# Value tiles and three query groups as three products of rounded parts; the held chunk's work ahead of the last batch's cross units

## What is computed

```python
x = x + _L0_attn_ref(_layernorm(x, axis=-1), L0_attn_wq, L0_attn_wk, L0_attn_wv, L0_attn_wo)
x = x + _L0_xattn_ref(_layernorm(x, axis=-1), ctx_512, L0_xattn_Wq, L0_xattn_Wkv_expand, L0_xattn_Wout)
x = x + _L0_ffn_ref(_layernorm(x, axis=-1), L0_ffn_w_gate, L0_ffn_w_up, L0_ffn_w_down)
```

```python
h = jax.nn.silu(jnp.einsum('bsh,hi->bsi', x, w_gate)) * jnp.einsum('bsh,hi->bsi', x, w_up)
h_sparse = _sparsify_2to4(h)
return jnp.einsum('bsi,ih->bsh', h_sparse, w_down)
```

## Time and profile before

| | us |
|---|---|
| median of 3 executions | 415.29 (414.1 to 415.61) |
| the profiled execution, whole | 414.97 |
| its span, first to last instruction | 413.2 |
| PE busy | 392.2 (95% of the span) |
| DVE busy | 286.0 (69%) |
| ACT busy | 211.2 (51%) |
| POOL busy | 161.2 (39%) |

### The profile page before, as it was taken

How to read it: one execution, slowest core, us unless ns; L and a number is a source line. 1 busy time by engine, 2 the same in 40 slices (tenths; PEclk the granted TensorE clock), 3 DMA queues, 4 the chain that set the end, 5 groups by cost and what they waited for, 6 DMA issues and landing times.

```text
span 413.2 us, 7990 instructions
## 1 busy us (share of the span) xinstructions
PE 392.2 (95%) x2959; PEld 317.1 (77%) x2960; DVE 286.0 (69%) x607; ACT 211.2 (51%) x537; POOL 161.2 (39%) x160
## 2 busy tenths in 40 slices
PE   8997999899999999999999999999998999889996
PEld 7776778667699777777789877877786879757895
DVE  5977931788769972688859974688959961585373
ACT  1574731587334841486443752287544741777230
POOL 5562790378411420277611430167632500255000
PEclk9999999999999999999999999999999999988999
DMA  7985430303001300242000400342001300300000
GB/s 214 367 309 149 121 103 33 118 24 78 3 6 52 103 0 27 79 121 78 0 8 2 153 2 2 102 110 64 2 2 66 87 2 27 110 19 2 27 0 27
DMA packets 33446, 28.90 MB, mean 70 GB/s; under 512 B 18688, under 2 KB 28032, under 8 KB 33152
## 3 DMA queue, kind: packets, MB, share of 16 engines
q1 hardware_dynamic: 33408, 28.40, 22.2%
HBM read 19.21 MB, written 5.24 MB: 59 GB/s over the span
## 4 chain that ended last, share of the span: by engine, by line
PE 65%; DVE 16%; issue 6%; ACT 5%; POOL 4%; DMA 2%; SPq 1%; POOLq 0%; DVEq 0%; ACTq 0%
PE ps L593 13%; PE ps L462 13%; PE ps L658 9%; PE ps L534 8%; PE ps L674 3%; DVE mx L909 3%; PE ps L555 3%; PE ps L579 3%; PE ps L471 3%; ACT prob L1264 3%; POOL prob L1158 3%; DVE total L923 2%; PE ps L514 2%; PE ps L632 2%; DMA wqk_sb<-in_wqk 2%
## 5 line engine op out<-in xcount | busy, mean ns | idle before, releaser
L1158 POOL TENSOR_TENSOR prob<-prob,inv 128x512 f32<-128x512 f32 x80 | 84.4, 1060 | 84.6 <-DVE inv L929 84.5
L462 PE MATMUL ps<-xnT,wqk_sb 128*128 128x256 f32 x320 | 77.4, 384 | 1.1 <-DMA wqk_sb<-in_wqk 0.8
L462 PEld LDWEIGHTS ps<-xnT,wqk_sb 128*128 128x128 f32 x320 | 57.8, 190 | 11.6 <-issue 3.8
L1264 ACT ACTIVATE prob<-ps,mx 128x128 f32<-128x128 f32 (+1 forms) x128 | 52.5, 426 | 15.8 <-DVE mx L907 14.7
L1151 POOL TENSOR_TENSOR qs<-rope 128x512 f32<-128x512 f32 x32 | 40.7, 1271 | 43.1 <-DVE rope L879 39.1
L534 PE MATMUL ps<-ident_sb,prob 128*128 128x128 f32 x320 | 50.3, 282 | 5.2 <-POOL prob L1158 5.0
L1274 ACT ACTIVATE pT<-ps 128x512 f32<-128x512 f32 x80 | 47.6, 599 | 13.7 <-PE ps L534 13.2
L879 DVE TENSOR_TENSOR rope<-ps,trig_sb 64x512 f32<-64x512 f32 x70 | 48.2, 688 | 0.9
L534 PEld LDWEIGHTS ps<-ident_sb,prob 128*128 128x128 f32 x320 | 37.9, 143 | 13.2 <-POOL prob L1158 8.4
L1134 POOL TENSOR_TENSOR rstd<-vareps,power 128x1 f32<-128x1 f32 x24 | 13.2, 553 | 76.7 <-DVE vareps L858 76.5
L907 DVE TENSOR_REDUCE mx<-ps 128x2 f32<-128x512 f32 (+1 forms) x48 | 32.7, 689 | 10.0 <-PE ps L514 9.4
(11 more groups left out here) (145 smaller groups left out, 693.9 us busy)
## 6 DMA issues: line engine op xcount, KB each, us to landing
k<-kx SPq DMA_DIRECT2D x32, 128.0 KB, 2.9
q<-qx SPq DMA_DIRECT2D x32, 128.0 KB, 2.6
vb<-v_sb SPq DMA_DIRECT2D x42, 64.0 KB, 2.1
wqk_sb<-in_wqk SPq DMA_DIRECT2D x4, 512.0 KB, 8.2
work<-in_wgu SPq DMA_DIRECT2D x4, 512.0 KB, 9.6
wo_sb<-in_wo SPq DMA_DIRECT2D x1, 2048.0 KB, 15.7
vb<-v_sb SPq DMA_DIRECT2D x36, 32.0 KB, 2.4
wd_sb<-in_wd SPq DMA_DIRECT2D x1, 1024.0 KB, 6.1
```

The source lines that it names most:

```text
L462: mm = pe.matmul(o[:, half, :], wqk_sb[:, k, g, half, :], xnT[:, 0, k, :], start=(k == 0), stop=(k == KT - 1))
L1158: pool.tensor_tensor(p, p, inv[:, i % ND, 0:g].unsqueeze(2).broadcast_to([P, g, 512 // g]), ALU.mult).then_inc(s_norm, 1)
L1264: ins = act.activation(prob[:, i % ND, h * k:(h + 1) * k], ps[:, BANK_S + i % 2, h * k:(h + 1) * k], ACT.Exp, bias=mx[:, i % ND, h:h + 1], ...
```

## The change

**Three products.** From the second batch on, that is wherever b is not `None`, `v_tile` and the query groups 5, 6 and 7 (`SPLIT`) are computed in three products of float32r parts. The parts of the rows, `xs_hi` and `xs_lo`, lie in the buffers of the latent keys. ACT writes `xs_hi` and then `xnT` (`rows_parts`, in the place of `copy_norm`); DVE subtracts (`rows_rest`, behind `rank_sums` and ahead of `keep`, in batch 0 behind `normalise`). The parts of the weights are made in batch 0: five rounding copies on ACT (`half_weights`, one after each of the exponentials 3 to 7) and five subtractions on POOL (`rest_of_weights`), two ahead of the last four `split_weights` and three behind them.

**Held chunk.** In the last batch "up10" is multiplied between the scores of units 1 and 2 of the window (code of the batch before), gate and up of "11" ahead of `cross_norm(b, 0)`; DVE's comparisons and `keep` stand ahead of the cross units; `down(HELD, 0)` is done ahead of them and half of `down(HELD, 1)` after the second. Two and two `idle` products take places between the units. DVE copies the transposed probabilities of the first four cross units. A one-column exponential moves ACT's table load ahead.

**Space.** The context is loaded into both halves of the partitions, the two latent weights share a tile, and both window outputs lie in `qs`; the comparisons of the held chunk lie in `pT`.

```diff
+SPLIT = (5, 6, 7)
-IDLE = {"values": 1, "transposes": 1, "gates": 1, "ranks": 3, "last": 1}
-HELD_FIRST = {2: (1, 2), 4: (3,)}
-HELD_SECOND = {13: (0,), 14: (1,)}
+IDLE_UNITS = {13: 1, 14: 1}
+IDLE = {"scores": 2, "values": 1, "transposes": 1, "gates": 1, "ranks": 3, "last": 1}
+HELD_AT = 2
...
                 for half in halves:
+                    if b is not None and g in SPLIT:
...
+                        for k in range(KT):
+                            pe.matmul(o[:, half, :], wq_hi[:, k, j, half, :], xs_hi[:, k, :], start=(k == 0), stop=False)
+                            pe.matmul(o[:, half, :], wq_lo[:, k, j, half, :], xs_hi[:, k, :],
+                                      start=False, stop=False)
+                        for k in range(KT):
+                            mm = pe.matmul(o[:, half, :], wq_hi[:, k, j, half, :], xs_lo[:, k, :],
+                                           start=False, stop=(k == KT - 1))
...
                 if more:
-                    wait_drained(pe, "ln1", b)
                     v_tile("v0", b, 0)
                     window_out(b, 1, pair=0)
                 else:
-                    for j in range(2):
-                        gate_up(HELD, 1, j, ("gate",))
+                    gate_up(HELD, 1, 0, ("gate",))
+                    gate_up(HELD, 1, 1)
                 cross_norm(b, 0, n)
...
                 if not more:
-                    for j in range(2):
-                        gate_up(HELD, 1, j, ("up",))
+                    down(HELD, 0, (0, 1, 2))
                 cross_norm(b, 1, n)
...
                     if not more:
-                        if i in HELD_FIRST:
-                            down(HELD, 0, HELD_FIRST[i])
+                        if i == HELD_AT:
+                            down(HELD, 1, (0, 1))
+                        if i == HELD_AT + 1:
+                            wait_drained(pe, "up11", HELD)
+                            idle(IDLE["scores"], BANK_O)
...
                 if b == HELD:
-                    for i in range(HEAD):
-                        unit_scores(b + 1, i)
+                    unit_scores(b + 1, 0)
+                    unit_scores(b + 1, 1)
+                    gate_up(HELD, 1, 0, ("up",))
+                    unit_scores(b + 1, 2)
...
+                if c and b < HELD:
+                    rows_rest(b + 1)
                 dve.wait_ge(s_wins, FC * b + c + 1)
...
+            def unit_pT(b, i):
+                u = UNITS * b + i
+                dve.wait_ge(s_tr, u + 1)
+                dve.wait_ge(s_av, u - NPT + 1)
+                dve.tensor_copy(pT[:, i % NPT, :], ps[:, BANK_PT + i % 2, :]).then_inc(s_pTv, 1)
...
                 if b == 0:
+                    for k in range(KT):
+                        rest_of_weights(k)
                     for c in range(NQB - LATE, WCHUNKS):
                         split_weights(c)
+                    for k in range(len(SPLIT)):
+                        rest_of_weights(KT + k)
                 n = 3 * b + (3 if more else 2)
                 inverse_root(1, n, (0,))
...
+            def rows_parts(b):
+
+                wait_filled(act, "ln1", b)
+                act.wait_ge(s_kx, 32 * (b + 1))
+                act.activation(xs_hi[:], half_banks("ln1", b), ACT.Copy)
+                act.activation(xnT[:, 0], half_banks("ln1", b), ACT.Copy).then_inc(s_xhi, 1)
```

212 lines of the change are left out of this document (139 added, 73 removed).

## The result

The changed kernel took **421.12 us** (417.42 to 422.71, four executions) beside 415.21 of the kernel before: a ratio of 1.0138, with a 95% interval of 1.0103 to 1.0173. That is slower by 1.4%, and outside the predicted range, 412.8 to 419.2. The same kernel, measured three more times beside the kernel before, gave 1.0046 (1.0014 to 1.0077), 1.0082 (1.0064 to 1.0100) and 1.0077 (1.0047 to 1.0106), with medians of 417.49, 417.76 and 417.75. So two things have to be explained: the 3 us or so by which it is slower in most executions, and the 3.6 us more of the first measurement.

A forecast was written before the change was run, and what follows sets the result against it. PE was taken to bound the middle batches, while in the last batch's cross units it waits for ACT's exponentials. Sum: 414.97 − 2.2 + 3.8 + 1.3 − 1.15 = 416.7 us; range 412.8 to 419.2.

The forecast's parts named there:

- The products: Value tiles and query groups in batches 0 to 2 as three products of parts: −2.2 us, bounds 0 and −4.5.
- the groups: Query groups 5, 6 and 7 as products of parts: 0.55 us gained in each of three batches, −1.65.
- the value tiles: Value tiles as products of parts in batches 0 to 2: −0.75 us from v1, +0.2 cost at v0.
- v0: First value tile, before the first cross norm: gain nil, rows late, cost +0.1 us in batches 1 and 2.
- q7's second half: Second half of the last query group: only covers DVE's last normalisation, lands nothing; the first half lands 0.15 us.
- q5: Query group ahead of the transposes of units 9 and 10: gives 0.1 of its 0.30 us.
- q6: Query group covering ACT copies that move with PE: its 0.30 us lands in full.
- POOL's queue: Batch 0: nine subtractions delay the second norm's inverse root, so PE waits at `cross_norm(0, 0)`: +3.8 us, bounds 0 and 5.4.
- if PE finds rows ready there: Sign of being wrong: PE not waiting for DVE's rows at `cross_norm(0, 0)` in batch 0, where some 4 us idle was forecast.
- The clock behind the stall: Batch 0, after PE's wait: a stretch at 1.2 GHz costs +1.3 us, bounds 0 and 3.4.
- The last batch: Held chunk reordered, ACT paces the cross units: −1.95 us plus 0.8 for the clock, −1.15; bounds +0.8 and −3.5.
- slower by the second query tile: Rival: before the fifth cross unit, DMAs a microsecond later keep PE at 1.2 GHz; 419.1 us, chance 0.25.

The follow-up runs named there:

- seven_guarded: The guarded kernel: changed kernel, seven of POOL's nine subtractions moved behind the second norm's inverse root, POOL waiting for DVE before each piece; 410.12 us, 0.9887.
- groups_alone: seven_guarded with the value tiles back in float32, so only q5, q6 and q7 are products of parts; 412.01 us, 0.9919.
- root_first: Changed kernel, POOL's nine subtractions in batch 0 start only when DVE has normalised the next batch's rows; 418.39 us, 1.0092.
- before_seven: Kernel before, three more subtractions into unread tiles behind POOL's four in batch 0; 416.30 us, 1.0024.
- seven_behind_root: Changed kernel, seven of POOL's nine subtractions in batch 0 moved behind the second norm's inverse root, no waits added; 410.69 us, 0.9922.
- four_first: Changed kernel, POOL's nine reordered: the four of the gate weights first, then the two value parts and three of the query groups; 415.52 us, 1.0024.
- eight_lookups: Changed kernel, eight more SBUF to SBUF normalisations on DVE in batch 0 against POOL's nine subtractions, into unfilled tiles; 421.02 us, 1.0133.
- other_form: Changed kernel, DVE's normalisation of the second row tile of the next rows in batch 0 also writes its row sum to a spare tile; 417.97 us, 1.0094.
- after_third: Changed kernel without edit, measured a third time; 417.76 us, 1.0082.
- after_fourth: Changed kernel without edit, measured a fourth time; 417.75 us, 1.0077.
- guarded_again: seven_guarded without edit, measured again for its spread; 410.52 us, 0.9908.
- before_guarded: Kernel before, POOL's four subtractions of batch 0 held until DVE has normalised the next rows; 414.49 us, 0.9995.

## Why the prediction was wrong, and where it was right

*The products, −2.2.* Measured −2.0. The parts lay otherwise: the groups gave 1.05 where I had 1.65, and the value tiles 0.95 where I had 0.75 − 0.2 = 0.55. Of the value tiles, v0 gave nothing, as predicted: in batch 1 the first cross norm stands 33.34 us behind the start of the batch before and 33.36 in the guarded kernel. But it waits 0.04 us there and not 0.3, nothing beyond v0's own gain is lost, and in batch 0 the value tiles gave 0.29 where I had 0.15. (A wait of 0.33 us did appear, for 0.17 before, but at the last normalisation of each batch, where q7's second half lands nothing, as predicted.)

Of the groups, in batch 1 of groups_alone q5 gave 0.11 (predicted 0.1), q7 0.16 (0.15) and q6 0.10 where I had 0.30; three times that 0.2 is the missing 0.6. I had written that q6 covers copies by ACT that move with PE. Its second half covers one that doesn't move with it. The last transposes, ACT's copy and the values behind q6, before and in seven_guarded:

```profile
200.86 0.65 PE L534 MATMUL ps<-ident_sb,prob 128*128 128x128 f32 x4
201.56 0.60 ACT L1274 ACTIVATE pT<-ps 128x512 f32<-128x512 f32 x1 [1.38 <-PE ps L534]
202.31 0.64 PE L579 MATMUL ps<-pT,v2z 128*32 128x128 f32 x16
...
199.79 0.66 PE L603 MATMUL ps<-ident_sb,prob 128*128 128x128 f32 x4
200.49 0.60 ACT L1388 ACTIVATE pT<-ps 128x512 f32<-128x512 f32 x1 [1.26 <-PE ps L603]
201.23 0.65 PE L649 MATMUL ps<-pT,v2z 128*32 128x128 f32 x16
```

From the transposes to the values it is 1.45 us before and 1.44 after, and both times the values start 0.15 us behind the end of the copy. The copy sets this stretch, so shorter products between them give nothing. The middle batches got 0.6 us shorter, not 0.8.

*POOL's queue, +3.8.* Right to a tenth in place, length and releaser, in three profiles of the changed kernel (3.82, 3.85, 3.85), and the three runs that lengthen or move its cause agree: root_first, before_seven, seven_behind_root. In the one profile of the first measurement this wait doesn't exist, because a longer one stands in front of it. That is one of the prediction's own signs of being wrong, "if PE finds rows ready there".

*The clock behind the stall, +1.3.* Too small. Batch 0 took 97.9 to 99.1 us in the three later profiles, 5.6 to 6.8 above the 92.35 of the guarded kernel; less the wait of 3.85 that is 1.7, 1.9 and 2.9 us. The windows behind the stall show it, in the columns of the earlier trace rows, above for the second measurement of after, below for root_first:

```profile
68.10:76.00 7.90, 7.88 (x34) 6.93 (x35) 0.42 (x1) 0.77 (x2) 0.00 (x0) 0.78 0.10 33
...
69.20:77.00 7.80, 7.70 (x28) 6.78 (x29) 0.42 (x1) 0.77 (x2) 0.00 (x0) 0.64 0.03 10
```

A mean of 0.78 over 7.9 us is 3.5 us at 1.2 GHz, one stretch as I had assumed, in which PE loses half of what it works: 1.75 (1.9 by the stages). A mean of 0.64 over 7.8 us is 5.6 us, and half of it 2.8. PE is busy throughout, so nothing hides the half speed. I had taken 1.3 of the 1.7 that one stretch can cost; it was 1.7 to 2.9.

*The last batch, −1.15.* Measured −1.4 and −1.5 at like clocks, and up to −2.9 where the clock had fallen in the profile of before and not in that of after. The steps: the first cross score 1.3 later than the rest (predicted 1.4), the wait for the second query tile 2.25 us (predicted 2.5), seven units of ACT in 9.8 us (predicted 10.3; 11.3 and 11.4 in the two profiles of after whose clock fell there):

```profile
365.49 0.38 PE L579 MATMUL ps<-mask_sb,ident_bf 128*128 128x512 bf16 x1
...
373.40 0.27 PE L579 MATMUL ps<-mask_sb,ident_bf 128*128 128x256 bf16 x1 [2.25 <-DMA q<-qx]
...
389.76 1.13 PE L711 MATMUL ps<-xwo_sb,o2T 128*128 128x256 f32 x4
```

*The sum.* With the measured terms: 414.97 − 2.0 + 3.85 + 1.7 to 2.9 − 1.4 = 417.1 to 418.3, and the later medians are 417.5 to 417.8. The prediction's 416.7 is short of that by what the clock was undersized.

*The step that failed* is the path in the part on POOL: there the queue's length reaches PE only through the inverse root. I asked who waits for POOL's queue by semaphores, and took DVE's normalisation from the earlier trace rows as 0.41 us. The row of before that spoke against it was not looked at, the pair of normalisations ahead of it:

```profile
55.45 1.87 DVE L866 TENSOR_SCALAR xn<-x_buf,moments,rstd 128x256 f32<-128x256 f32 x2 [3.13 <-POOL rstd L1134]
```

It takes 1.87 us, and not the 0.93 of root_first, because its second half lies beside POOL's first subtraction. Whoever sees that asks what nine in a row do to it. In most executions the answer is "the same as four". In the profiled execution of the first measurement it was 11.11 us for one instruction and 8.71 for PE, 4.9 more than the wait that I had forecast; with it batch 0 took 103.10 us and not 98 to 99. This is read from one profile. That POOL's queue held DVE out there is an inference from two facts: the instruction ended with the queue, and beside POOL this form otherwise takes up to 1.36 us, alone 0.41. Why DVE didn't get its turn for nine operations is open. It was not met again in eleven other profiles in which the same two instructions meet (before and its variants among them), and no experiment brought it back. None of the rivals had it; the nearest in time was "slower by the second query tile" (419.1), whose mechanism didn't appear in any profile of after: that tile's first score came 2.0 to 2.3 us after PE was ready, about as forecast.

The second step is a size: the clock behind the stall, put at 1.3 us, measured at 1.7 to 2.9. It is what lifts even the later medians above the forecast.

## What to carry to other kernels

Work that is moved onto POOL has two kinds of waiters: those behind a semaphore, and DVE instructions that read and write SBUF beside it. Look for DVE instructions that are longer than their kind beside POOL's, and put POOL's long pieces behind the last thing that PE needs from either engine; here moving seven instructions by one place turned 0.5 to 0.8% slower (1.4% in the first measurement) into 0.8 to 1.1% faster. Behind a long wait in front of a full PE, count the clock as well: 1.7 to 2.9 us behind 3.8 to 4.4 here. Two waits of the same sum, 2.50 and 1.30 us, cost nothing beyond themselves in four_first.

## What the runs showed of the hardware

A normalisation from SBUF to SBUF on DVE (128x256, 0.41 us alone) that meets a subtraction of POOL takes up to 1.36 us; eight in a row against nine of POOL's each took 1.35 to 1.36 (eight_lookups), strictly in turns, and slowed POOL by 0.04 us a piece. The same instruction with an accumulator took 0.54 (other_form). Once the plain form took 11.11 us, for nine operations of POOL (after, first measurement).

PE's granted clock fell to 1.2 GHz at a wait of 3.8 to 4.4 us in all seven profiles that had one. In five of them it was low for 3.4 us of work behind the wait; in after_third and root_first it fell 0.9 and 1.3 us before PE went on, and stayed low for 5.9 and 5.5 us of work. It did not fall at waits of 2.50 and 1.30 us with 3.4 us of work between them. At the wait for the second query tile, 2.0 to 2.3 us, it fell in 8 of 15 profiles, and the length doesn't tell in which: it did at 2.12 (after_fourth) and not at 2.29 (guarded_again). In the kernel before it fell twice in the last batch, behind waits of 1.17 and 0.99 us, and in before_guarded, with 1.06 and 0.99, not at all.
